# Gated delta rule: the decay matrices from two-row products in four row tiles, masked by VectorE's minimum instead of by GpSimd's multiply

## The reference, cut to what matters

```python
def step(state, xs):
    q_t, k_t, v_t, g_t, b_t = xs
    state = state * jnp.exp(g_t)[..., None, None]
    kv = jnp.einsum('bhk,bhkv->bhv', k_t, state)
    delta = (v_t - kv) * b_t[..., None]
    state = state + jnp.einsum('bhk,bhv->bhkv', k_t, delta)
    out = jnp.einsum('bhk,bhkv->bhv', q_t, state)
    return (state, out)
```

## Time and profile before

| | us |
|---|---|
| median of 3 runs | 1787.74 (1787.28 to 1789.94) |
| the profiled execution | 1803.65 |
| its span (first to last instruction) | 1802.1 |
| PE busy | 1571.8 (87% of the span) |
| DVE busy | 1033.7 (57%) |
| POOL busy | 800.1 (44%) |
| ACT busy | 771.8 (43%) |
| mean granted TensorE clock | 0.937 |

### The profile page before, as it was taken

One profiled execution on the slowest core, in us unless ns is written; L12 is line 12 of the kernel. 1 busy time (PEld: TensorE's weight loads), 2 busy tenths in 40 slices (PEclk: granted clock), 3 DMA queues, 4 the chain that ended last, 5 costly groups with the idle time before them and its releaser, 6 DMA issues. The chain is left out here.

```text
span 1802.1 us, 27445 instructions
## 1 busy us (share of the span) xinstructions
PE 1571.8 (87%) x9790; PEld 1149.2 (64%) x9790; DVE 1033.7 (57%) x2127; ACT 771.8 (43%) x1745; POOL 800.1 (44%) x1336
## 2 busy tenths in 40 slices
PE   3749999999999999999999999986979995978860
PEld 2436777777777777777778778764547764635540
DVE  4426677677777777777777777553035555312323
ACT  1325565565565565565565655541124331100110
POOL 0367667656656756757657657100000000061326
PEclk9779999999999999999999999998989996789995
DMA  4111111111111111111111111004210001023424
GB/s 154 38 27 26 32 38 28 36 33 30 39 33 30 34 33 36 33 33 36 34 33 37 33 33 23 8 10 197 112 30 1 1 1 53 1 85 86 144 86 116
DMA packets 119087, 84.41 MB, mean 47 GB/s; under 512 B 92658, under 2 KB 104518, under 8 KB 118192
## 3 DMA queue, kind: packets, MB, share of 16 engines
q1 hardware_dynamic: 112304, 64.73, 13.1%
q0 software_dynamic: 6656, 18.01, 3.3%
HBM read 63.00 MB, written 20.05 MB: 46 GB/s over the span
## 5 line engine op out<-in xcount | busy, mean ns | idle before, releaser
L580 PE MATMUL psum_banks<-main_hT,heads_w_in 128*128 128x512 f32 x512 | 248.7, 612 | 19.1 <-DVE heads_y L882 11.0
L882 DVE SCALAR_TENSOR_TENSOR heads_y<-psum_banks,gdn_conv_w,heads_y 128x1021 f32<-128x1021 f32 (+2 forms) x192 | 244.7, 1275 | 28.4 <-ACT heads_y L756 27.4
L1069 POOL TENSOR_TENSOR heads_XT<-heads_XT,heads_tmp 128x126 f32<-128x126 f32 (+22 forms) x496 | 207.1, 418 | 38.9
L1066 POOL TENSOR_TENSOR heads_tmp<-heads_XT,heads_A 128x126 f32<-128x126 f32 (+22 forms) x496 | 184.0, 371 | 38.9
L1604 POOL DMA_INDIRECT expert_rows<-moe_xn,route_dest x32 | 31.4, 981 | 365.5 <-issue 365.5
L580 PEld LDWEIGHTS psum_banks<-main_hT,heads_w_in 128*128 128x128 f32 x512 | 93.9, 196 | 94.8 <-issue 69.4
L667 PE MATMUL psum_banks<-heads_w_z,main_hT 128*128 128x256 f32 x512 | 126.6, 392 | 0.0
L693 PE MATMUL psum_banks<-heads_w_o,heads_ogT 128*128 128x256 f32 x512 | 119.2, 381 | 2.9 <-ACT heads_ogT L818 1.0
L756 ACT ACTIVATE heads_y<-psum_banks,gdn_conv_w 128x1024 f32<-128x1024 f32 x64 | 71.3, 1114 | 114.2 <-PE psum_banks L580 114.2
L778 ACT ACTIVATE heads_Dt<-heads_Dl,gdn_coef 128x128 f32<-128x128 f32 x224 | 77.4, 393 | 90.7 <-DVE heads_Dl L895 89.3
L1053 POOL TENSOR_TENSOR heads_Dm<-heads_Dm,main_upto 128x512 f32<-128x512 f32 x64 | 87.0, 1380 | 52.8 <-ACT heads_Dm L816 52.8
(11 more groups left out here) (249 smaller groups left out, 3511.0 us busy)
## 6 DMA issues: line engine op xcount, KB each, us to landing
main_w_gu<-in_w_gu SPq DMA_DIRECT2D x4, 2816.0 KB, 24.9
heads_w_in<-in_w_in SPq DMA_DIRECT2D x16, 512.0 KB
heads_A<-kk_blocks SPq DMA_DIRECT2D x64, 128.0 KB, 2.6
moe_wd<-in_w_down POOLq DMA_DIRECT2D x32, 176.0 KB, 2.7
expert_rows<-main_zeros SPq DMA_DIRECT2D x1, 4096.0 KB, 14.5
heads_w_z<-in_w_z SPq DMA_DIRECT2D x16, 256.0 KB, 2.7
heads_w_o<-in_w_o SPq DMA_DIRECT2D x16, 256.0 KB, 2.7
inverse_blocks<-heads_XT SPq DMA_DIRECT2D x32, 128.0 KB, 2.9
```

The lines of the kernel that those rows point to most:

```text
L580: ins = pe.matmul(out[:, half * 512:(half + 1) * 512], w_in[:, kd_, j * P:(j + 1) * P], hT[:, kd_, half * 512:(half + 1) * 512], start=kd_ ...
L882: dve.scalar_tensor_tensor(y[j][:, shift:T], src[:, 0:T - shift], conv_w[:, head, j, t:t + 1], y[j][:, shift:T], ALU.mult, ALU.add).then_i ...
L1066: pool.tensor_tensor(tmp[:, 0:n, 0:m], bc_last(XT[:, 0:n, j], m), bc_mid(A0[:, j, j + 1:BLK], n), ALU.mult).then_inc(solve_step.sem, 1)
L1069: pool.tensor_tensor(XT[:, 0:n, j + 1:BLK], XT[:, 0:n, j + 1:BLK], tmp[:, 0:n, 0:m], ALU.add).then_inc(solve_step.sem, 1)
```

## The change

The running sums, `diff`, and their negatives are now turned so that the tokens lie along the free dimension (two more transposes on PE and two copies on DVE in `gate_coefficients`), stored to memory and, per head, loaded as rows: `row_to` has the row of sums over a row of ones, `row_from` a row of ones over the row of negated sums, at partitions 32g and 32g+1 for unit g. The product of the two two-row operands is then cum_i - cum_j. The four units of a head are made together, at k=8, as 16 products of 128x128 with two rows each, unit g in row tile g and bank g. DVE takes the minimum with `limit` (a large positive number for j <= i, a large negative one elsewhere) from PSUM into `Dm` and frees the bank; ACT takes the exponential in place. POOL's two operations per unit go, and so does the constant `after`.

```diff
 PLAN:
-    [("p2", None), ("decay0", 1)],
-    [("p3", None), ("decay1", 2), ("decay2", 0)],
-    [("decay3", 0)],
+    [("p2", None)],
+    [("p3", None)],
+    [("decay0", 0), ("decay1", 1), ("decay2", 2), ("decay3", 3)],
     [("kk0", 1), ("kk1", 3), ("v3", 0)],

 gate_coefficients, SP:
+                sp_.wait_ge(s_ct, 2)
+                for sign in range(2):
+                    sp_.dma_start(cum_dram[sign].rearrange("(half p) t -> p half t", p=P), cum_t[:, sign]).then_inc(s_cstore, 16)
                 sp_.wait_ge(s_in[3], 16)
                 sp_.wait_ge(s_in[4], 16)
                 sp_.wait_ge(s_bload, 64)
+                sp_.wait_ge(s_cstore, 32)
 gate_coefficients, PE:
+                pe.wait_ge(s_v, 11)
+                for half in range(2):
+                    ins = pe.transpose(turned[:, 2 + half], diff[:, half * P:(half + 1) * P], consts["ident"][:])
+                ins.then_inc(s_cturned, 1)
 gate_coefficients, DVE:
                 dve.tensor_copy(diff[:], cum[:, 0:HK * IT]).then_inc(s_v, 1)
+                dve.wait_ge(s_cturned, 1)
+                dve.tensor_copy(cum_t[:, 0], turned[:, 2:4]).then_inc(s_ct, 1)
+                dve.tensor_scalar(cum_t[:, 1], turned[:, 2:4], -1.0, None, ALU.mult).then_inc(s_ct, 1)

 heads, tiles:
-    gU = [a.sb(f"gU{g}", [P, 4, P]) for g in range(4)]
+    row_from = [a.sb(f"row_from{i}", [P, 4, P]) for i in range(2)]
+    row_to = [a.sb(f"row_to{i}", [P, 4, P]) for i in range(2)]
+    limit = a.sb("limit", [P, P])
 heads, SP:
+            def gate_rows(h):
+                for sign, rows in enumerate([row_to, row_from]):
+                    src = cum_rows[sign, IT * h:IT * (h + 1)].rearrange("(g s) t -> g s t", g=4)
+                    sp.dma_start(rows[h % 2][sign:P:32], src).then_inc(s_rows[h % 2], 16)
...
             weights("w_o", w_o_ready, 0, w_o)
+            sp.wait_ge(s_ones, 4)
+            gate_rows(0)
+            gate_rows(1)
...
                     weights("w_z", w_z_ready, h, w_z)
                 if h + 2 < HK:
+                    sp.wait_ge(full[BANK["decay3"]].sem, full[BANK["decay3"]].done(h, "decay3"))
+                    gate_rows(h + 2)
                     sp.wait_ge(pair_full.sem, pair_full.done(h, "3"))
 heads, PE:
-                elif name.startswith("decay"):
-                    pe.wait_ge(gu_ready.sem, gu_ready.done(h, str(u)))
+                elif name == "decay0":
+                    pe.wait_ge(s_rows[par], 32 * (h // 2 + 1))
+                    for g in range(1, 4):
+                        more = free[BANK[f"decay{g}"]]
+                        wait(pe, more, more.ahead(h, f"decay{g}"))
...
-                if name not in ("y6b", "u6b"):
+                if name not in ("y6b", "u6b", "decay1", "decay2", "decay3"):
                     wait(pe, free[b], free[b].ahead(h, name))
...
-                elif name.startswith("decay"):
-                    pe.matmul(flat(bank[b][:]), after[:], flat(gU[u][:]), start=True, stop=True).then_inc(full[b].sem, 1)
+                elif name == "decay0":
+                    for s in range(4):
+                        for g in range(4):
+                            r, out = slice(32 * g, 32 * g + 2), bank[BANK[f"decay{g}"]]
+                            ins = pe.matmul(out[:, s], row_from[par][r, s], row_to[par][r, s], start=True, stop=True)
+                            if s == 3:
+                                ins.then_inc(full[BANK[f"decay{g}"]].sem, 1)
 heads, ACT:
+                if name.startswith("decay"):
+                    act.wait_ge(free[b].sem, free[b].done(h, name))
+                    part = flat(Dm[:, 4 * u:4 * u + 4])
+                    act.activation(part, part, ACT.Exp).then_inc(dm_ready.sem, 1)
+                    return
...
-                elif name.startswith("decay"):
-                    if u == 0:
-                        wait(act, uf_ready, uf_ready.base(h))
-                    act.activation(flat(Dm[:, 4 * u:4 * u + 4]), flat(bank[b][:]), ACT.Exp).then_inc(free[b].sem, 1)
 heads, DVE (evacuate):
+                elif name.startswith("decay"):
+                    dve.wait_ge(full[b].sem, full[b].done(h, name))
+                    dve.tensor_tensor(Dm[:, 4 * u:4 * u + 4], bank[b][:], bc_mid(limit[:], 4), ALU.min).then_inc(free[b].sem, 1)
 heads, POOL:
-            def columns_of_g(h, g):
...
-                pool.tensor_tensor(gU[g][:], bc_mid(upto[:], 4), bc_last(src, P), ALU.mult).then_inc(gu_ready.sem, 1)
-            def mask_decay(h, g):
...
-                pool.tensor_tensor(part, part, bc_mid(upto[:], 4), ALU.mult).then_inc(dm_ready.sem, 1)
...
+            for i in range(2):
+                pool.memset(row_from[i][:], 1.0).then_inc(s_ones, 1)
+                pool.memset(row_to[i][:], 1.0).then_inc(s_ones, 1)
+            pool.tensor_scalar(limit[:], upto[:], 1e30, -1e30, ALU.mult, ALU.add).then_inc(s_limit, 1)
             pool.wait_ge(s_own, 16)
-            for g in range(4):
-                columns_of_g(0, g)
...
-                if h in INVERT:
-                    for g in range(4):
-                        mask_decay(h, g)
                 if h in AHEAD:
-                    for g in range(4):
-                        columns_of_g(h + 1, g)
```

More of the change, by code:

```diff
@@ L276, in gated_delta @@
         S = a.sb("S", [P, HD, P])
-        gate_coefficients(nc, a, hT, consts, d, coef, conv_w, gamma, powers, minus_half, beta_rows)
+        cum_rows = gate_coefficients(nc, a, hT, consts, d, coef, conv_w, gamma, powers, minus_half, beta_rows)
         with ExitStack() as inner:
-            heads(nc, Alloc(nc, inner, "heads", a), x, hT, consts, d, coef, conv_w, gamma, powers, minus_half, S, beta_rows)
+            heads(nc, Alloc(nc, inner, "heads", a), x, hT, consts, d, coef, conv_w, gamma, powers, minus_half, S, beta_rows, cum_rows)
         a.clear_sems()
@@ L307, in gate_coefficients @@
         beta_t = a.sb("beta_t", [P, 2, P])
+        cum_t = a.sb("cum_t", [P, 2, 2, P])
+        cum_dram = nc.dram_tensor("cum_dram", (2, HK * IT, P), F32, kind="Internal").ap()
+        s_cturned, s_ct, s_cstore = a.sem("cum_turned"), a.sem("cum_turned_copied"), a.sem("cum_stored")
         beta_dram = nc.dram_tensor("beta_dram", (HK * HD * C, P), F32, kind="Internal").ap()
@@ L418, in _, with heads @@
                 dve.wait_ge(s_a, 7)
-def heads(nc, a, x, hT, consts, d, coef, conv_w, gamma, powers, minus_half, S, beta_rows):
-    ident, upto, after = consts["ident"], consts["upto"], consts["after"]
+        return cum_dram
+def heads(nc, a, x, hT, consts, d, coef, conv_w, gamma, powers, minus_half, S, beta_rows, cum_rows):
+    ident, upto = consts["ident"], consts["upto"]
     w_in = a.sb("w_in", [P, KD, 4 * P])
@@ L500, in heads @@
     q_root_ready = per_head("query_root_ready", "it")
-    gu_ready = per_head("g_columns_ready", "0", "1", "2", "3")
+    s_rows = [a.sem(f"gate_rows{i}_loaded") for i in range(2)]
+    s_ones, s_limit = a.sem("rows_of_ones"), a.sem("limit_written")
     dm_ready = per_head("decay_masked", "0", "1", "2", "3")
@@ L803, in evacuate @@
                     return
-                if not (name[0] in "zuy" or name[:2] in ("kk", "fl", "de")):
+                if not (name[0] in "zuy" or name[:2] in ("kk", "fl")):
                     return
@@ L1013, in _ @@
             block_scales(0)
+            dve.wait_ge(s_limit, 1)
             for h in STEPS:
@@ L1041, in _ @@
         def _(pool):
-            def columns_of_g(h, g):
[L1043 to L1046, removed]
-                pool.tensor_tensor(gU[g][:], bc_mid(upto[:], 4), bc_last(src, P), ALU.mult).then_inc(gu_ready.sem, 1)
-            def mask_decay(h, g):
-                b = BANK[f"decay{g}"]
-                pool.wait_ge(free[b].sem, free[b].done(h, f"decay{g}"))
-                part = Dm[:, 4 * g:4 * g + 4]
-                pool.tensor_tensor(part, part, bc_mid(upto[:], 4), ALU.mult).then_inc(dm_ready.sem, 1)
             def key_root():
@@ L1834, in _ @@
             sp.wait_ge(s_out, 16 * NT)
-CONSTS = ["ident", "upto", "after", "before"]
+CONSTS = ["ident", "upto", "before"]
 def load_constants(nc, a, d, x, buf, s_zeroed):
@@ L1845, in load_constants @@
         "upto": a.sb("upto", [P, P]),
-        "after": a.sb("after", [P, P]),
         "before": a.sb("before", [P, P]),
@@ L1915, in shape_constants @@
     f = np.float32
-    return {"ident": np.eye(P, dtype=f), "upto": (j <= i).astype(f), "after": (j > i).astype(f), "before": (j < i).astype(f),
+    return {"ident": np.eye(P, dtype=f), "upto": (j <= i).astype(f), "before": (j < i).astype(f),
             "own_row": own.astype(f)}
```

## The result

| | before | after |
|---|---|---|
| median, us | 1787.57 (4 runs) | 1859.77 (4 runs, 1852.22 to 1861.82) |
| profiled execution, us | 1803.65 | 1858.8 |
| mean granted clock | 0.937 | 0.908 |

The ratio is 1.0393, 95% interval 1.0362 to 1.0424: slower by 72 us. POOL's busy time went from 800.1 to 644.7 us, as the change says, and bought nothing.

The account below looks back on a forecast made before the run. PE was taken to bound the head loop, with DVE late at k=8 and 9. 14 steps of 3.8 us (53) plus 4.5, 1 and 1 gave 60 us; 1848 forecast against the 1787.74 median, range 1820 to 1875.

Parts of the forecast that it names:

- The likeliest case: Head loop, k=8 and 9: DVE's late minima hold PE back and its clock falls in most steps; 1848 us, chance 0.73.
- DVE's queue: At k=8 the minima stand behind X, normalize and turn_blocks, so kk0 waits and y6a comes 2.6 us later at full clock.
- the clock: PE's wait before kk0 drops it to 1.2 GHz in most steps: y6a 3.0 to 4.5 us late, taken as 3.8.
- a sum of 60: Whole kernel: 14 steps of 3.8 us make 53, plus 4.5, 1 and 1 in single terms, 60 us slower.
- PE's part: A head's four decay products, 3.44 us, become row-tiled two-row products of 1.0; by PE alone a step loses 2.44 us.
- The 2.6 us at full clock: Delay of y6a per step from the order of DVE's work, PE's own 2.44 us saving already included.
- One sign: Expected in the profile after, at k=7 to 9: DVE without a gap from the tap to v3.
- near 74: Step length in us expected in the profile after, against 70.12 in the earlier trace.
- Once each: Terms outside the 14 steps: step 0 +4.5 us, step 15 +1, gate_coefficients 0 to 2 taken as 1.
- PE's sum: Rival: DVE frees banks 1 and 3 before PE asks at kk0, PE keeps 2.44 us in 16 steps; 1750, chance 0.06.
- Full clock: Rival: DVE's order delays each step 2.6 us but the granted clock stays at 1.00; 1830 us, chance 0.12.
- The much slower case: Rival: decay products run one by one at 1.2 GHz, 6.9 us, second minimum 1.9 later; 1875 us, chance 0.06.

Follow-up runs that it names:

- unit-by-unit run: Kernel after the change, with PE's loops over units and matrices exchanged so a unit's four products follow each other in one row tile: 1856.22 us, ratio 1.0375.
- filler run: Kernel after the change, with seven idle 128x256 products on PE in the wait before kk0: 1836.85 us, ratio 1.0273.
- rearranged run: Kernel after the change, with decays at k=7, DVE's minima early, turn_blocks behind k=10's taps, exponentials behind kk1, z2 before y6: 1778.23 us, ratio 0.9984.
- old places: Kernel after the change, with the plan of before: each unit's two-row products at k=6, 7, 7, 8 in their former banks, minima spread likewise: 1836.54 us, ratio 1.0314.
- three rearranged kernels: Kernel after with decays and minima early, turn_blocks late (1778.23 us); that with norm_k at k=12 (1797.95); that with normalize 2 and 3 also later (1796.4).

## Why the prediction was right

**The size and the sign.** Forecast 1848 in 1820 to 1875, measured 1859.77. The likeliest case was the one that came, by the mechanism that it named: DVE's queue and, behind it, the clock. The loss is 72 us for a sum of 60, so some terms were too small, the clock's above all.

**PE's part.** 1.0 us was taken for the decays, 0.9 and 3.44 the ends; 1.17 measured, first start to last end. That it does not matter was shown by the unit-by-unit run (2.82).

**DVE's queue.** The layout was made on the clock of another step; shifted by the start of L639 at k=6 (645.24 there, 681.84 here, 36.60 apart) its points came at: p3 648.62 (648.54 forecast), X 652.95 (652.87), first minimum 656.25 (656.17), Dl 658.65 (658.57), kk0 657.68 (657.55). y6a came at 663.11, 3.7 late, where 3.8 was taken. The 2.6 us at full clock are those of the filler run. One sign did not come: DVE was to have no gap from the tap to v3, and it waits 2.66 us for v3's transposes, since kk0 and kk1 ahead of them on PE run at half the clock.

**The clock.** It fell in every step, not in most, for 6.8 us in each and in some a second time for 3.4. So the per-step price was larger than in the one step laid out: from `turn_blocks` to `turn_blocks` the twelve steps up to the fourteenth took (1068.27 - 239.69) / 12 = 69.05 us before and (1130.96 - 250.91) / 12 = 73.34 after, 4.3 against 3.8. Of this 2.5 is the queue's by the filler run, where 2.6 was taken, and 1.8 the clock's, where 1.2 was: this is the term that was too small. A slip lies beside it: the step of 70.12 us of the earlier trace rows is not the usual one. The clock had fallen once in it, at 602 us, for 3.4 us; the usual step was 68.7. So "near 74", which 73.34 seems to meet, is in part luck: 70.12 was 1.1 above the mean step, and 3.8 was 0.5 below the mean loss. The second falls behind norm_k and u6a, which the rearranged run brought up and which five of ten steps after have, were in the trace of before and were not seen.

**Once each.** Start: SP issues w_in 0.9 us later (1 forecast). Step 0: its length, from `turn_blocks` to the next, went from 56.42 to 62.27, 5.9 and not 4.5; the wait for the second minimum ends there at a clock of 0.50 (at 122.6 us; 98.0 to 135.5 are at 1.2 GHz). Step 15 and the last two: the final addition to x starts 69.5 us later than before, of which 67.5 were there at `turn_blocks` of step 15: 2 and not 1. In all 1.1 up to `turn_blocks` of step 0, 5.9 for step 0, 60.5 for 14 steps and 2 for the end: 69.5 for a forecast of 60. The spans differ by 55 only, since the other three layers took 570 us in that execution of before and 556 in that of after; the medians differ by 72.

**The rivals.** PE's sum (1750) fell with the first trace. Full clock (1830) describes the filler run, 1836.85, and not the kernel. The much slower case fell as the tiles do run side by side, and the unit-by-unit run, where they hardly do, is no slower.

**Two rules.** Four packed row tiles are 2.82 / 1.17 = 2.4 times as fast as the same products one tile after the other, and 3.44 / 1.17 = 2.9 times as fast as the full products that they replace. The Trainium skill (TensorE: Matmul & The Clock Gate, "Measured speedup vs the span model") has 3.07 for four row tiles; here it is less, and nothing hung on it. Evacuation was the limit, though not by DVE's total time, 57% of the span: by its order. The Trainium skill (TensorEngine Tiling (Array Packing), "PSUM Bottleneck") warns that the copy out of PSUM may become the limit once tiling has made TensorE faster, and this trace agrees with its 3.37 us wait for a minimum.

## What to carry to other kernels

Work taken off the engine that bounds is worth what the next release lets it keep: before moving an evacuation to another engine, write down what stands ahead of it in that engine's queue and who comes back for the bank. An engine at 57% can be the bound for five microseconds of each step, and reordering its queue was worth more here than any instruction saved. And count what an edit does to TensorE's clock: a part of the wait was paid a second time by the products behind it, 1.8 us a step.

## What the runs showed of the hardware that was not expected

- The granted clock fell although PE's records show no gap. With two-row products in place of products of all rows (same number, shape and place) there were 54.6 against 10.2 us at 1.2 GHz in 750 us. It also fell behind 16 records of one column followed by 96 of 32x32: three times before, six times rearranged, never with the two groups set apart by one quantum. The Trainium skill (TensorE: Matmul & The Clock Gate, "Why this matters for your kernels") ties the clock to idle gaps; these runs show it fall without one, and the measurement decides.
- Sixteen float32 products of 128x128 with two rows, in four row tiles over all 128 columns into four banks, take 1.17 us; one tile after the other 2.82. Four of them alone in one tile took 1.09 from start to start at the old places (739.06 to 740.15 us), where one product of all rows and the same 512 columns took 0.86.
- Idle products in a wait made a kernel 1.2% faster. In the two kernels with norm_k moved, the wait before kk0 and the falls are both gone without them.
- The other layers' 14 us between the two executions lie in one place: from the last addition to x at L121 (a normalized output) to the first one of the mixture of experts (L1592 before, L1619 after) it is 98.2 us before and 79.2 after. All thirteen profiled executions have either 79 to 81 us there (eight of them) or 95 to 99 (five), whatever the edit. What makes the difference stays open.
- The changed layer ends at 1220.7, 1222.0 and 1219.7 us in the profiles of the three rearranged kernels, against 1231.8 before. The medians show 0 to 7 us of these 10 to 12; why not all of it stays open too.
